# Mixing of attention heads in two row tiles, in an audio tower on one core

## What is computed

```python
dots = jnp.einsum('bhid,bhjd->bhij', q, k) * scale
attn = jax.nn.softmax(dots, axis=-1)
attn = jnp.einsum('bhij,hg->bgij', attn, reattn_w)     # mixing of heads
a = attn.transpose(0, 2, 3, 1)
mu = jnp.mean(a, axis=-1, keepdims=True)
var = jnp.mean((a - mu) ** 2, axis=-1, keepdims=True)
a = (a - mu) * jax.lax.rsqrt(var + LN_EPS) * ln_g + ln_b
attn = a.transpose(0, 3, 1, 2)
out = jnp.einsum('bhij,bhjd->bhid', attn, v)
```

## Time and profile before

| | |
|---|---|
| median of 3 runs | 666.47 us (666.38 to 666.81) |
| span of the profiled execution | 663.0 us |
| TensorE busy | 629.2 us, 95% of the span |
| VectorE busy | 475.8 us, 72% |
| ScalarE busy | 412.6 us, 62% |
| GpSimd busy | 340.5 us, 51% |
| mean granted TensorE clock | 0.992 of full speed |

### The profile page before, as it was taken

How to read it: one execution, slowest core, us unless ns; L and a number is a source line. 1 busy time by engine, 2 the same in 40 slices (tenths; PEclk the granted TensorE clock), 3 DMA queues, 4 the chain that set the end, 5 groups by cost and what they waited for, 6 DMA issues and landing times.

```text
span 663.0 us, 16042 instructions
## 1 busy us (share of the span) xinstructions
PE 629.2 (95%) x5715; PEld 560.5 (85%) x5715; DVE 475.8 (72%) x1416; ACT 412.6 (62%) x1378; POOL 340.5 (51%) x516
## 2 busy tenths in 40 slices
PE   8887799999999999999999999999999999999887
PEld 7777598998989898898989899898989989887665
DVE  4755867778686877778787777768777786867453
ACT  3476576657658576675757666675766676575400
POOL 2465447365554646465455647545474655546300
PEclk9999899999999999999999999999999999998999
DMA  6000020302103030300303020120303011020303
GB/s 222 25 2 24 2 93 24 104 26 69 60 2 126 3 104 24 104 27 21 109 1 105 25 104 25 38 92 2 107 22 105 24 65 42 8 98 1 104 0 116
DMA packets 23663, 37.37 MB, mean 56 GB/s; under 512 B 2272, under 2 KB 14496, under 8 KB 23584
## 3 DMA queue, kind: packets, MB, share of 16 engines
q1 hardware_dynamic: 23584, 36.35, 16.7%
HBM read 33.14 MB, written 3.20 MB: 55 GB/s over the span
## 4 chain that ended last, share of the span: by engine, by line
PE 87%; DVE 6%; ACT 3%; POOL 2%; issue 2%; ACTq 0%; DVEq 0%; POOLq 0%
PE ps_fill L421 14%; PE ps_mix L653 14%; PE ps_fill L423 12%; PE ps_fill L422 12%; PE ps_dots L642 9%; PE ps_av L661 7%; PE ps_fill L795 7%; PE ps_fill L582 7%; PE ps_fill L787 2%; DVE x2T_lo L1176 1%; PE ps_fill L769 1%; ACT x2T_hi L908 1%; PE ps_fill L770 1%; PE ps_dots L597 1%; PE ps_fill L712 1%
## 5 line engine op out<-in xcount | busy, mean ns | idle before, releaser
L1256 POOL TENSOR_TENSOR sum<-sq 92x384 f32<-92x384 f32 x64 | 64.5, 1007 | 123.7 <-ACT sq L831 123.7
L823 ACT ACTIVATE ex<-ps_dots,negmax 128x92 f32<-128x92 f32 x384 | 124.3, 342 | 3.6 <-DVE negmax L1092 3.2
L653 PE MATMUL ps_mix<-mixk,probs 128*92 128x128 f32 x768 | 97.7, 278 | 3.0 <-DVE aT L1113 2.7
L1250 POOL TENSOR_TENSOR probs<-ex,rinv 128x552 f32<-128x552 f32 x64 | 71.0, 1109 | 54.0 <-DVE rinv L1098 54.0
L653 PEld LDWEIGHTS ps_mix<-mixk,probs 128*92 128x92 f32 x768 | 87.2, 161 | 6.2 <-POOL probs L1250 2.6
L1197 DVE SCALAR_TENSOR_TENSOR act<-ps_fill,b_neg,spread 128x368 f32<-128x368 f32 x123 | 68.0, 592 | 21.9 <-PE ps_fill L423 16.4
L823 ACT ACTIVATION_READ_ACCUMULATOR ex<-ps_dots,negmax 128x1 f32 x384 | 81.3, 212 | 0.0
L642 PE MATMUL ps_dots<-xT,yT 128*64 128x92 f32 x1536 | 73.6, 245 | 3.0 <-ACT ex L823 3.0
L642 PEld LDWEIGHTS ps_dots<-xT,yT 128*64 128x64 f32 x1536 | 64.1, 137 | 6.1 <-ACT ex L823 3.8
L1111 DVE TENSOR_TENSOR aT<-ps_mix,arstd 92x360 f32<-92x360 f32 x128 | 61.7, 522 | 6.1 <-ACT arstd L841 3.8
L1131 DVE TENSOR_TENSOR oT_lo<-ps_av,oT_hi 128x368 fp32r<-128x368 f32 x64 | 34.6, 541 | 31.6 <-ACT oT_hi L869 31.2
(11 more groups left out here) (206 smaller groups left out, 1596.7 us busy)
## 6 DMA issues: line engine op xcount, KB each, us to landing
spread<-weights SPq DMA_DIRECT2D x64, 368.0 KB, 5.5
xin<-in_x SPq DMA_DIRECT2D x16, 320.0 KB
out<-ostage SPq DMA_DIRECT2D x16, 128.0 KB, 4.2
out<-ostage SPq DMA_DIRECT2D x16, 56.0 KB, 4.5
xin<-in_x SPq DMA_DIRECT2D x16, 52.0 KB
act<-w_raw SPq DMA_DIRECT2D x1, 576.0 KB, 6.7
w_sb<-w_raw SPq DMA_DIRECT2D x1, 576.0 KB, 7.9
qkv<-qk_raw SPq DMA_DIRECT2D x1, 512.0 KB, 5.5
```

The costliest lines, as they stand in the source:

```text
L653: last = pe.matmul(ps_mix[0:N, c // HALF, o:o + 128], probs[:, (s - 1) % 2, c, :], mixk[:, :, :].rearrange("p g i -> p (g i)"), start=True ...
L823: last = act.activation(ex[:, s % 2, c, :], ps_dots[:, c // HALF, o:o + N], ACT.Exp, bias=negmax[:, c:c + 1], accum_out=sums[:, s % 2, c:c ...
L1250: pool.tensor_tensor(probs[:, s % 2, :, :], ex[:, s % 2, :, :], rinv[:, s % 2, :].unsqueeze(2).broadcast_to([128, CHUNKS, N]), ALU.mult).t ...
L1256: pool.tensor_tensor(sum4[:, :, :, :], sq[:, :, 0:4, :], sq[:, :, 4:8, :], ALU.add)\
```

## The change

The 92 queries of a sequence now lie in six chunks exactly 16 apart, that is, 96 queries; the last four of a sequence are the first four of the next, or zeros behind the last one (the moving operand of the Y products grows from 368 to 372 columns, `WY`). The rows of a chunk go by half, head, query: two halves of 8 queries (`IR`), each with 64 rows (head, query). The mixing of a chunk becomes two matmuls, one for each half: 64 rows of `probs` with 64 rows of `mixk`, and 64 output columns. The first half's outputs go to one bank of `ps_mix`, the second's to the other. `mixk` is 128 x 64 instead of 128 x 128. Square, tree and `arstd` keep their element counts in the new order. VectorE's scaling is one product for each half, and `aT` has a stride of 96 a head.

```diff
-STARTS = [0, 15, 30, 46, 61, 76]
+WY = W + NS - N
+IR = IC // 2
...
-        mixk = sb("mixk", [128, HEADS, IC])
+        mixk = sb("mixk", [128, HEADS, IR])
...
-        yT = sb("yT", [128, 2 * SLOTS, HALF, HEADS, IC])
+        yT = sb("yT", [128, SLOTS, 2 * CHUNKS, HEADS, IR])
...
-        aT = sb("aT", [N, 2, HEADS * N])
+        aT = sb("aT", [N, 2, HEADS * NS])
...
                     for c in range(CHUNKS):
                         o = NS * (c % HALF)
-                        rows = yT[:, 2 * PLACE[s] + c // HALF, c % HALF, :, :].rearrange("p h i -> p (h i)")
                         for r in range(0, 128, DH):
-                            last = pe.matmul(ps_dots[r:r + DH, c // HALF, o:o + N], rows[:, r:r + DH],
+                            rows = yT[:, PLACE[s], 2 * c + r // DH, :, :].rearrange("p h i -> p (h i)")
+                            last = pe.matmul(ps_dots[r:r + DH, c // HALF, o:o + N], rows,
                                              xT[:, N * PLACE[s]:N * PLACE[s] + N], start=True, stop=True)
...
                     for c in range(CHUNKS):
-                        o = 128 * (c % HALF)
-                        last = pe.matmul(ps_mix[0:N, c // HALF, o:o + 128], probs[:, (s - 1) % 2, c, :],
-                                         mixk[:, :, :].rearrange("p g i -> p (g i)"), start=True, stop=True)
+                        for half in range(2):
+                            rows = slice(DH * half, DH * half + DH)
+                            last = pe.matmul(ps_mix[0:N, half, DH * c:DH * c + DH], probs[rows, (s - 1) % 2, c, :],
+                                             mixk[rows, :, :].rearrange("p g i -> p (g i)"), start=True, stop=True)
                     last.then_inc(mix_ready, 1)
...
-                    products(ps[:, 0:W], [a[:, int(step[1]), :] for a in A], [m[:, 0:W] for m in xT_split])\
+                    products(ps[:, 0:WY], [a[:, int(step[1]), :] for a in A], [m[:, 0:WY] for m in xT_split])\
...
-                to = aT[:, (s - 1) % 2, 0:HEADS * N].rearrange("p (g n) -> p g n", n=N)
-                mixed = ps_mix[0:N, :, 0:128 * HALF].rearrange("p a (c g i) -> p a c g i", c=HALF, g=HEADS)
-                scale = arstd[:, :, :].rearrange("p (a c) i -> p a c i", a=2)
-                row = STARTS[1]
-                for a in range(2):
-                    dst = bass.AP(tensor=to.tensor, offset=to.offset + STARTS[HALF * a],
-                                  ap=[list(to.ap[0]), [row, HALF], [N, HEADS], [1, row]])
-                    dve.tensor_tensor(dst, mixed[:, a, :, :, 0:row],
-                                      scale[:, a, :, 0:row].unsqueeze(2).broadcast_to([N, HALF, HEADS, row]), ALU.mult)
-                dve.tensor_tensor(to[:, :, STARTS[HALF] - 1::STARTS[HALF]].rearrange("p g a -> p a g"),
-                                  mixed[:, :, HALF - 1, :, row],
-                                  scale[:, :, HALF - 1, row].unsqueeze(2).broadcast_to([N, 2, HEADS]), ALU.mult)\
-                   .then_inc(aT_ready, 1)
+                to = aT[:, (s - 1) % 2, :].rearrange("p (g c r i) -> p r c g i", g=HEADS, c=CHUNKS, r=2)
+                mixed = ps_mix[0:N, :, 0:DH * CHUNKS].rearrange("p r (c g i) -> p r c g i", c=CHUNKS, g=HEADS)
+                scale = arstd[:, :, :].rearrange("p (r c) i -> p r c i", r=2)
+                for half in range(2):
+                    last = dve.tensor_tensor(to[:, half, :, :, :], mixed[:, half, :, :, :],
+                                             scale[:, half, :, :].unsqueeze(2).broadcast_to([N, CHUNKS, HEADS, IR]),
+                                             ALU.mult)
+                last.then_inc(aT_ready, 1)
```

More of the change, by code:

```diff
@@ L46, in table_columns @@
 def table_columns():
-    widths = [("ident", 128), ("vecT", 12), ("gate", E), ("ln_g", HEADS), ("ln_b", HEADS // 2), ("diag16", IC),
+    widths = [("ident", 128), ("vecT", 12), ("gate", E), ("ln_g", HEADS), ("ln_b", HEADS // 2), ("diag16", IR),
               ("mixw", HEADS), ("b2", 128), ("rev", TILES * E)]
@@ L315, in audio_tower @@
         probs = sb("probs", [128, 2, CHUNKS, N])
[L316 to L321, removed]
-        aT = sb("aT", [N, 2, HEADS * N])
+        sq = sb("sq", [N, 2 * CHUNKS, HEADS, IR])
+        sum4 = sb("sum4", [N, 2 * CHUNKS, 4, IR])
+        sum2 = sb("sum2", [N, 2 * CHUNKS, 2, IR])
+        sumsq = sb("sumsq", [N, 2 * CHUNKS, IR])
+        lnvar = sb("lnvar", [N, 2 * CHUNKS, IR])
+        arstd = sb("arstd", [N, 2 * CHUNKS, IR])
+        aT = sb("aT", [N, 2, HEADS * NS])
         oT = split("oT", [128, HEADS // 2, SLOTS, N])
@@ L461, in chunked @@
         def chunked(ps):
-            whole = ps[:, 0:W]
+            whole = ps[:, 0:WY]
             return bass.AP(tensor=whole.tensor, offset=whole.offset,
-                           ap=[list(whole.ap[0]), [STARTS[HALF], 2 * SLOTS], [STARTS[1], HALF], [1, IC]])
+                           ap=[list(whole.ap[0]), [N, SLOTS], [IR, 2 * CHUNKS], [1, IR]])
         def patches(ps):
@@ L661, in attention @@
                         last = pe.matmul(ps_av[o:o + DH, NS * (g // 2):NS * (g // 2) + N],
-                                         v_sb[:, (s - 2) % SLOTS, DH * g:DH * g + DH], aT[:, s % 2, N * g:N * g + N],
+                                         v_sb[:, (s - 2) % SLOTS, DH * g:DH * g + DH], aT[:, s % 2, NS * g:NS * g + N],
                                          start=True, stop=True)
@@ L831, in square @@
                 act.activation(sq[:, :, :, :].rearrange("p (a c) g i -> p a (c g i)", a=2),
-                               ps_mix[0:N, :, 0:128 * HALF], ACT.Square).then_inc(sq_ready, 1)
+                               ps_mix[0:N, :, 0:DH * CHUNKS], ACT.Square).then_inc(sq_ready, 1)
             def attention_rstd(b):
@@ L991, in prepare @@
                     dve.wait_ge(prep, 3)
-                    dve.tensor_tensor(mixk[:, :, :], diag16.unsqueeze(1).broadcast_to([128, HEADS, IC]),
-                                      mixc[:, :].unsqueeze(2).broadcast_to([128, HEADS, IC]), ALU.mult)\
+                    dve.tensor_tensor(mixk[:, :, :], diag16.unsqueeze(1).broadcast_to([128, HEADS, IR]),
+                                      mixc[:, :].unsqueeze(2).broadcast_to([128, HEADS, IR]), ALU.mult)\
                        .then_inc(mixk_ready, 1)
@@ L1320, in layouts @@
             ("ln_b", np.repeat(ln_b.reshape(4, 2).T, DH, axis=0)),
-            ("diag16", np.tile(np.eye(IC), (HEADS, 1))),
-            ("mixw", np.repeat(reattn_w, IC, axis=0)),
+            ("diag16", np.tile(np.eye(IR), (2 * HEADS, 1))),
+            ("mixw", np.tile(np.repeat(reattn_w, IR, axis=0), (2, 1))),
             ("rev", np.broadcast_to(np.tile(np.arange(E, 0, -1), TILES), (128, TILES * E)))]:
```

## The result

| | before | after |
|---|---|---|
| median of 5 runs | 666.47 us (664.95 to 666.81) | 660.40 us (657.89 to 662.62) |
| ratio of the times | | 0.9905, 95% interval 0.9885 to 0.9926 |
| span of the profiled execution | 663.0 us | 658.6 us |
| mean granted clock | 0.992 | 0.980 |

The kernel became 0.95% faster: 6.1 us by the medians, 4.4 by the two profiled spans. The forecast was 8.1, so the question is where the rest went. (The two granted clocks are those of the profiled executions.)

The account below looks back on a forecast made before the run. TensorE, busy 95%, was taken to bound the kernel. A mixing gain of 9.3 us less 0.7 for Y products and 0.5 for new waits gave 8.1: span 654.9, median 658 us, range 651 to 668.

Parts of the forecast that it names:

- The mechanism: Mixing on TensorE: two row tiles overlap loads and streams, gaining 0.58 us a group, 9.3 us over sixteen.
- Pairs: Two mix matmuls, one in each row tile: a pair every 0.080 us, set by the 92-column load.
- out of a mix: Edge from the last mix matmul to the first of what follows: 0.15 us, last stream 0.054 plus 0.093 lost.
- the Y columns: Y products on TensorE stream 372 columns instead of 368: 0.0018 us more each, 0.7 us in all.
- the new waits: Allowance of 0.5 us in all for waits that might appear behind the shorter mixes.
- The argument against one rule: Rule: loads overlap matmuls only in another row group. Against it: full-array mix at 0.109 us, load 0.080, stream 0.107.
- The other edits: Y products cost 0.7 us; VectorE's scaling, two products of 546 ns, saves 8 us off the path; nothing counted for it.
- short runs: GpSimd's tree: its runs halve, but the rows show no price on that; VectorE would hide one.
- Rival 1: More gain in the mix: loads cost nothing, 0.29 us a mix, 18 us in all, 640 us; chance 0.05.
- Rival 2: Slower inside the mix: pairs don't overlap in full, 0.108 to 0.160 us a pair, 678 to 714 us; chance 0.11.
- Rival 3: No change: five more tiling changes a group at 0.12 us more each, or new waits, 664 to 667 us; chance 0.12.
- Rival 4: Slower: granted clock falls to 0.50, 3.4 us a stretch; one in every second group gives 685 us; chance 0.05.

Follow-up runs that it names:

- experiment 1: Kernel after, but the mixing issues the six matmuls of the first half, then the six of the second, instead of alternating: 702.02 us (one run).
- experiment 2: Kernel after with only the row tiling undone, one 128-row, 128-column product a chunk with zeros in `mixk`: 667.12 us, ratio 1.0011 to the kernel before.
- experiment 11: Kernel after with 68 of the 92 keys mixed from the second sequence on, so loads have 68 columns: 653.04 us (one run).
- experiment 12: Kernel after with full-array mixing for the first seven sequences and row tiles from the eighth on: 658.64 us, ratio 0.9896 to the kernel before.

## Why the prediction was right, and where it was not

- **The mechanism: right.** Pairs at 0.082 us against 0.080; 0.17 out of a mix against 0.147; a steady group 37.5. The median lies 2.4 us over the 658.0 forecast, inside its range. The working gives 8.1/16 = 0.51 us a group with the Y columns and the new waits in it, the trace 0.50. That loads and streams of two row tiles overlap was read from `pA0`, `pA1` and `dots`, and experiments 1, 2 and 11 bear out each part: the overlap, the tiling alone, the load (or the rows written with it) as the pace. The argument against one rule gives a stream of 128 columns 0.107 us; no row shows that figure, only the 0.109 between starts.
- **The other edits: right.** Scaling 546 ns, as worked out; no price on short runs on GpSimd; Y products 0.17 apart for 372 columns against 0.165. All of it together is nothing in experiment 2.
- **Rival 1 (loads cost nothing): refuted** by the pair and by experiment 11. The Trainium skill, "TensorE: Matmul & The Clock Gate", Part 3, "Measured speedup vs the span model", gives packed tiles one matmul's time and some 4 ns for each further one. The trace comes near it on the step inside a pair (7 ns) and disagrees on the pace of pairs: 0.082 us, where a stream of 64 columns would take 0.054, half of the 0.109 before.
- **Rival 2 (pairs don't overlap): refuted**, and experiment 1 shows the size of such a loss: 702, with most of the overlap gone.
- **Rival 3 (edges and new waits): refuted.** Each way out of a mix costs some 0.02 us more than worked out, and no wait was added in steady groups; the 0.5 us kept for them were not needed there.
- **Rival 4 (the clock): true in part, and the term that was missing from the sum.** The prediction placed it in steady groups, where no stretch is below 1.00, and gave it 0.05. It came in the first two iterations, where TensorE already stood idle: 13.7 us more at half the clock. They should have gained 1.0 us by the working; with the clock held they gain 0.6 (`dots` at 87.72 and 87.16), without that they lost 4.3. So the clock cost some 4.8, or 0.35 for each us at half, not the 0.5 put down. TensorE is busy in 17.8 of the 20.5 us, so part of it is waiting anyway; the rest of that difference was not followed up. The 71 runs of the kernel before beside the experiments agree: by a straight line, 0.01 of the mean clock (13.3 us at half) goes with 4.9 us, 0.37 for each. At the medians (0.989 before, 0.982 after) that is 3.5 us. Why the clock falls for longer after the change stays open (experiment 12). The profile of before showed the warning: its own stretch at 0.50, in those same iterations, and the idle TensorE ahead of it.
- **The ledger.** Predicted span 654.9, measured 658.6: 3.7 too little. The first two groups are 5.3 worse than worked out, 4.8 of it the clock; the other fourteen and the end gained 8.6 instead of 7.1, 1.5 better (0.9 of it behind the last group's first `dots`, not followed up).
- **From span to median.** The section on the time before puts all 3.5 us between them around the span; about half of it lies there. Each run's time is 1.7 to 1.9 above its own span (660.40 and 658.6; 702.02 and 700.1), so the profiled execution of before took some 664.8, a quick one, 1.7 under its median (its clock is 0.992, the median of the 71 runs 0.989). The forecast of the median doesn't suffer: 658.4 is 666.47 less 8.1. But the two profiled spans show 1.7 too little of the gain (4.4 for 6.1), and of the ledger's 3.7 that is 1.7; by the medians the gain is 2.0 short.

## What to carry to other kernels

Two products on half the rows each, issued in turn into two banks (one bank was not tried), replaced a full one at the price of the longer of load (0.080) and half stream (0.054); look at the load first, and count two edges of about 0.1 us. After a change that shortens TensorE's work, read the granted clock of the thin stretches (start and end) before anything else: here they took back between a third and nearly half of the gain, and 42 matmuls on zeros, placed where they wait for no late eviction, returned 7.5 us. An instruction moved for the sake of one engine may have been the cover of another's eviction.

## What the runs showed of the hardware that was not expected

- TensorE's look-ahead into another row tile is short: with twelve matmuls of one tile in a row, only the last three overlap with the other tile, by the spacing of the starts (1.65 us from first to last start, against 0.95 in turns).
- The same idle time ahead of the same work (1.65 and 1.67 of 3.43 us) was followed by 1.00 of the clock in one kernel and by 0.50 in another. Within one kernel the mean clock differs from run to run, and the time with it: after, 657.89 us at 0.984 and 662.62 at 0.979; before, 663.76 at 0.994 and 668.55 at 0.986. So the clock goes with the spread of the runs, and a profiled run should be read with its own clock. The Trainium skill, "TensorE: Matmul & The Clock Gate", Part 1, "What's actually happening", says that the gate looks at activity in windows that run freely beside the program; no run here shows them, but that alike stretches go both ways agrees with it.
